# Edge layers of a graph network: the second product of a group one turn later on TensorE

## What is computed

```python
def _mlp(h, W1, b1, W2, b2, g, beta):
    h = jax.nn.silu(h @ W1 + b1)
    h = jax.nn.silu(h @ W2 + b2)
    mu = jnp.mean(h, axis=-1, keepdims=True)
    var = jnp.mean(jnp.square(h - mu), axis=-1, keepdims=True)
    return g * (h - mu) * jax.lax.rsqrt(var + LN_EPS) + beta

for l in range(2):
    msg_in = jnp.concatenate([x[dst], x[src], edge_attr], axis=1)
    edges_new = _mlp(msg_in, eW1[l], eb1[l], eW2[l], eb2[l], eg[l], ebeta[l]) + edge_attr
    agg = jax.ops.segment_sum(edges_new, dst, num_segments=N_NODES)
    x = _mlp(jnp.concatenate([x, agg], axis=1), nW1[l], ...) + x
    edge_attr = edges_new
```

## Time and profile before

| | us |
|---|---|
| median of three runs | 4343.94 (4342.17 to 4346.43) |
| the profiled execution | 4335.36 |
| its span, first to last instruction | 4333.6 |
| granted TensorE clock, mean of the span | 0.798 |
| PE / DVE / ACT / POOL busy over the span | 73% / 59% / 31% / 49% |

### The profile page before, as it was taken

One profiled execution on the slowest core, in us unless ns is written; L12 is line 12 of the kernel. 1 busy time (PEld: TensorE's weight loads), 2 busy tenths in 40 slices (PEclk: granted clock), 3 DMA queues, 4 the chain that ended last, 5 costly groups with the idle time before them and its releaser, 6 DMA issues. The chain is left out here.

```text
span 4333.6 us, 75781 instructions
## 1 busy us (share of the span) xinstructions
PE 3180.2 (73%) x18633; PEld 2208.0 (51%) x18633; DVE 2559.6 (59%) x9494; ACT 1355.3 (31%) x2970; POOL 2130.8 (49%) x2173
## 2 busy tenths in 40 slices
PE   2488884669999997499998589998555555655554
PEld 1366662226666664377777367776333333333332
DVE  7678885986555563688887667776632222422223
ACT  0077875950111100255555345555300000200000
POOL 0477771000000001377775277776357777177776
PEclk7588987999999998599999799999755555755555
DMA  2112222000000002366666254455121212422223
GB/s 59 41 55 69 75 67 103 2 7 24 17 16 17 17 15 67 107 169 181 179 181 141 65 150 129 130 132 109 26 64 53 53 53 53 136 53 53 53 53 52
DMA packets 248988, 327.58 MB, mean 76 GB/s; under 512 B 78191, under 2 KB 159678, under 8 KB 247806
## 3 DMA queue, kind: packets, MB, share of 16 engines
q1 hardware_dynamic: 180410, 206.68, 15.5%
q0 software_dynamic: 68256, 117.02, 12.5%
HBM read 230.66 MB, written 92.83 MB: 75 GB/s over the span
## 5 line engine op out<-in xcount | busy, mean ns | idle before, releaser
L2520 PE MATMUL gat_acc<-gat_rows,gat_hot 128*128 128x128 f32 x1664 | 574.6, 478 | 486.0 <-issue 245.4
L2520 PEld LDWEIGHTS gat_acc<-gat_rows,gat_hot 128*128 128x128 f32 x1664 | 400.3, 317 | 661.6 <-issue 660.9
L992 PE MATMUL hop_p_a<-hop_h,adj 128*128 128x384 bf16 x4375 | 712.9, 327 | 0.0
L992 PEld LDWEIGHTS hop_p_a<-hop_h,adj 128*128 (+1 forms) x4375 | 428.5, 98 | 284.1 <-issue 1.7
L1928 POOL DMA_INDIRECT lb_far<-far_rows,lb_idx x416 | 405.6, 975 | 195.8 <-issue 117.0
L2503 POOL DMA_INDIRECT gat_rows<-typed_rows,gat_idx x416 | 395.7, 951 | 214.0 <-DVE gat_idx L2528 87.6
L2503 POOL DMA_INDIRECT gat_rows<-hidden_rows,gat_idx x416 | 395.2, 950 | 196.8 <-PE gat_acc L2520 77.4
L1928 POOL DMA_INDIRECT la_far<-far_rows,la_idx x416 | 409.7, 985 | 154.4 <-issue 117.9
L1650 POOL DMA_INDIRECT by_src_records<-scatter_rec,scatter_rank x375 | 376.9, 1005 | 128.9 <-issue 102.4
L2536 DVE TENSOR_SCALAR gat_hot<-iota_row,gat_tabs 128x128 f32<-128x128 f32 x416 | 147.7, 364 | 370.5 <-PE gat_acc L2520 364.4
L2533 DVE TENSOR_SCALAR gat_hot<-iota_row,gat_tabs 128x128 f32<-128x128 f32 x416 | 124.6, 305 | 392.6 <-PE gat_acc L2520 382.5
(11 more groups left out here) (498 smaller groups left out, 6418.9 us busy)
## 6 DMA issues: line engine op xcount, KB each, us to landing
edge_features<-emb_out SPq DMA_DIRECT2D x104, 256.0 KB
la_feat<-edge_features SPq DMA_DIRECT2D x104, 256.0 KB
edge_features<-la_out SPq DMA_DIRECT2D x104, 256.0 KB
lb_feat<-edge_features SPq DMA_DIRECT2D x104, 256.0 KB
la_place<-dst_row SPq DMA_DIRECT2D x104, 128.0 KB
lb_place<-dst_row SPq DMA_DIRECT2D x104, 128.0 KB
typed_rows<-gat_typed_row SPq DMA_DIRECT2D x25, 512.0 KB
hop_side<-x0share_nodes SPq DMA_DIRECT2D x125, 64.0 KB, 1.8
```

The costliest lines, as they stand in the source:

```text
L992: ins = nc.tensor.matmul(p_a[(u.par + r) % 2][:, 0:3 * D], K.adj[:, s, bass.ds(u.t * P, P)], h3[r % 2][:, s, :, :].rearrange("p i d -> p ( ...
L2520: nc.tensor.matmul(acc[:, bass.ds(at[u % LOADS], D)], hot[u % HOTS][:, :], rows[u % RING][:, :], start=False, stop=True, skip_group_check= ...
```

## The change

In PE's loop of edge_pass, second moves. Before, a turn was first(g), third(g-6), second(g). Now it is first(g), second(g-1), third(g-6). No instruction is added or removed, and no other engine's list is touched. The kernel calls edge_pass twice, so both layers change.

```diff
                         at = tile_offsets(nc, mybir.EngineType.PE, tile_row, g)
                     first(g, at)
+                if 1 <= g <= GE:
+                    second(g - 1)
                 if g >= SUM_LAG:
                     third(g - SUM_LAG)
-                if g < GE:
-                    second(g)
```

## The result

| | before | after |
|---|---|---|
| median of the runs, us | 4345.18 (4 runs) | 4677.44 (4673.94 to 4684.2, 4 runs) |
| the profiled execution, us | 4335.36 | 4676.02 |
| its span, us | 4333.6 | 4674.2 |
| granted TensorE clock | 0.798 | 0.808 |

The ratio is 1.0772, with a 95% interval of 1.0755 to 1.0788: +332 us by the medians, where +310 us had been forecast.

A forecast was written before the change was run, and what follows sets the result against it. PE and POOL's gathers were taken as about equally full, 5.0 to 5.1 us a group. Rounds of 6.72 and 6.67 us add 155.1 us in each layer: 4343.9 + 310 = 4654 us, range 4565 to 4715 us.

The forecast's parts named there:

- The removed cover: PE's second product finds hid ready long before; gain at most the 1.6 us of waits for hid, taken as nothing.
- The closed loop: Second product, rows, moments, one-hots, aggregates, next spread, near and feat matmuls form one loop that sets the pace; chance 0.78.
- The length of a round: Sum of five distances from second product to second product: 1.51 + 2.32 + 0.45 + 1.48 + 0.91 = 6.67 us.
- near to feat: On PE, start of near matmuls to start of feat product: 1.48 us, the mean where PE had waited for spread.
- feat to the next step: On PE, start of the feat product to the start of the next step: 0.91 us of the round.
- DVE in time: First layer: after roots, outs and add, DVE reaches bn_stats 0.18 us late once in four groups, 0.05 us a group.
- The near matmuls: PE's twelve matmuls ahead of feat, claimed to take 1.48 us after a wait for spread, 1.15 us otherwise.
- rival (a): Loop holds, but near matmuls aren't slowed by the wait: 4587 us, or 4490 us with the fastest; chance 0.10.
- The clock: PE's granted clock might fall because PE idles 1.2 to 1.6 us in every round; the main sum had no fall.
- rival (b): PE's clock falls, 1.5 us more a round: 4957 us, or 4715 us with a fifth of groups; chance beyond that 0.07.
- the prediction's last sign of being wrong: The granted clock in the layers is below 1.00 in the profile after the change.
- Starts and tails: Start and tail of each layer shift by less than one round each, in both directions; left at nothing.

## Why the prediction was right

**The removed cover** was worth nothing where the kernel before takes some 4340 us: the wait for hid was 1.6 us, and with the loop open the new order is 4 us slower, not faster.

**The closed loop** was the cause. Opening it in two ways took away 290 us and practically all of the loss; work added outside of it, no more than the stall could hold, cost nothing; work taken from two of its links shortened the kernel.

**The length of a round**, term by term, medians over the rounds of both layers: second product to rows 1.51 us (1.51 forecast); rows to spread 2.30 (2.32); spread to near 0.46 (0.45); near to feat 1.48 in the first layer and 1.44 in the second (1.48). Only feat to the next step was off: 1.01 us in place of 0.91. The 0.91 us came from a row in which the sums followed; now it is the bias of the second product. The weight load of the bias starts only with its matmul, with PEld idle for 0.76 us before it. The first one of the sums had started at 2719.97 us, while feat was on and 0.42 us ahead of its matmul. The row of the sums is from the kernel before, that of the bias from the changed one:

```profile
2719.97 0.19 PEld L1965 LDWEIGHTS lb_p_s<-lb_n,lb_hot 128*128 128x128 f32 x1 [0.24 <-issue]
...
2829.23 0.09 PEld L1974 LDWEIGHTS lb_p_m<-lb_b2r,ones_bf 3*128 3x128 bf16 x1 [0.76 <-issue]
```

Over 202 rounds that is 20 us; the rounds at the lower clock, below, add some 10 us. The other terms and the first rounds, with small differences in both directions, take some 3 us off, which gives the 27 us by which 337 exceeds 310. This one term was the largest error of the sum. Why the load of the bias isn't early was not tested. A duration read before the change is that of a step with its follower, not of the step alone.

**DVE in time**: in the first layer a late turn in each batch was forecast to cost 0.18 us, 0.05 us a group. Each fourth round takes 6.82 us in the median, the others 6.74 to 6.77 us: some 0.07 us a batch, 0.02 us a group. That the first layer's rounds are longer in the median than the second's (6.78 and 6.72 us) comes in the main from near to feat, 1.48 and 1.44 us, and not from DVE; the 6.72 us put on the first layer were near to the measured ones partly by luck.

**The near matmuls** (rival (a)) were the term with the widest bounds, 0.67 to 1.48 us. It was right to take the three rows whose wait stood in the same place, and the run with fixed addresses shows the reason that was given. In a group that found everything ready, with the near matmuls at 1839.82 us, the kernel before started feat 0.67 us later:

```profile
1840.49 1.08 PE L1950 MATMUL la_p_z<-la_feat,la_w 128*128 128x512 f32 x2
```

**The clock** (rival (b)) fell in a few rounds, where the sum had none: the mean is 0.98 from 2720 to 3320 us in the second layer, so the prediction's last sign of being wrong came true in a small way, and 0.99 in the first layer, as in the kernel before. Of the changed kernel's second layer, two rounds:

```profile
2867.23 1.60 PE L1947 MATMUL lb_p_z<-lb_spread,lb_near 128*128 128x128 bf16 x12 [1.46 <-DVE lb_spread L2045]
...
2873.94 1.72 PE L1947 MATMUL lb_p_z<-lb_spread,lb_near 128*128 128x128 bf16 x12 [1.46 <-DVE lb_spread L2045]
...
2875.45 2.02 PE L1950 MATMUL lb_p_z<-lb_feat,lb_w 128*128 128x512 f32 x2
2877.41 0.60 PE L1974 MATMUL lb_p_m<-lb_b2r,ones_bf 3*128 3x512 bf16 x1
```

and the busy time and granted clock around them (the clock is the third number from the end, 1.00 being 2.4 GHz and 0.50 1.2 GHz):

```profile
2868.00:2872.00 4.00, 4.00 (x28) 2.85 (x28) 0.60 (x3) 0.81 (x2) 1.79 (x3) 1.00 0.56 131
2872.00:2876.00 4.00, 2.54 (x18) 1.86 (x17) 2.96 (x14) 1.89 (x5) 2.73 (x3) 0.87 0.34 71
2876.00:2880.00 4.00, 4.00 (x12) 2.16 (x11) 0.00 (x0) 0.00 (x0) 1.43 (x2) 0.50 0.35 103
```

A stall of 1.46 us, like all the others, and then the feat product takes 1.96 us to its follower instead of 1.01. The round is 8.87 us long. After the first ten groups there are four such rounds in the second layer and one in the first, 2.1 us each, where rival (b) had put 1.5 us on one: some 10 us. In the run with the doubled sums, where the stall is shorter, no round after the first ten is longer than 7.0 us. The four rounds of the second layer are 8.4 us and cover the 7.5 us above; the other rounds are 0.05 us longer there (median 6.77 us).

The length of the stall doesn't decide by itself. In the run with fixed addresses PE stalls as long in the second layer, and the clock stays at 1.00 (from 2600 to 3200 us, waits and busy time):

```profile
PE lb_p_z L1947 <- DVE lb_spread L2045: 150.9, 101, 2.3
...
2600.00:3200.00 600.00, 448.79 (x3494) 326.00 (x3494) 372.21 (x1729) 266.64 (x590) 398.83 (x403) 1.00 0.48 111
```

That is 1.49 us in each round of 5.9 us. What decides which rounds are hit stays open. The rule of the Trainium skill named with rival (b) (TensorE: Matmul & The Clock Gate, section A second HAM failure mode: psum-queue depth-cycling) tells of such a swing between the two levels. The changed kernel's trace agrees in kind, at one round in forty and not as a swing of the whole layer; the second layer with fixed addresses doesn't show it.

**Starts and tails**, left at nothing, were 4 us.

## What to carry to other kernels

When a step moves in one engine's list, follow what it feeds through the lists of the other engines until the way comes back: here a product that was moved to hide one short wait closed a loop over three engines, because VectorE makes the input of the next group behind the moments of the last. The length of the loop is a sum of starts read off the timeline, and here it was the new pace as soon as it exceeded the old one; what lay outside of it cost nothing as long as it fitted into the stall. If such an order is wanted, move the prefetch first (one buffer more, one group earlier), and price each step with the follower that it will have.

## What was not expected of the hardware

- Twelve matmuls with addresses from registers take 0.67 us where everything was ready before them and 1.44 to 1.48 us right behind a wait; with fixed addresses it is 0.68 us behind the same wait. The register work is 0.8 us that a wait just ahead of it lays bare.
- With a stall of 1.46 us in every round the clock fell in about one round in twenty-five of the second layer, where a single stall of 1.67 us had left it alone. With the stall filled by useless products these rounds were gone, and they were absent too with fixed addresses, whose stall was as long (1.49 us in the mean).
- The same kernel took 4338 to 4345 us on some chips and 5272 to 5277 us on others, with POOL's gathers as long as ever but spaced by a wait that the profile doesn't name. The new order with doubled sums loses 7.7% on the one and 1.5% on the other; with the spread two groups ahead it loses 0.2% on the one and gains 0.4 to 0.6% on the other. Such a comparison holds for the kind of chip that it was made on.
